# The second payload copy of a scatter moved from GpSimd, in halves, to ScalarE, in one instruction

## The chip, the cores and the metric

The kernel runs on one core of a Trainium2 chip. Its engines work side by side, each with its own queue of instructions: TensorE (matmul, PE in the profile), VectorE (DVE), ScalarE (ACT), GpSimd (POOL) and SyncE (SP), which issues most DMAs. The metric is the device time of one execution in microseconds.

## The reference

A macaron layer: a mixture-of-experts feed-forward block, tiled attention, and the same feed-forward block again, on 16 x 512 tokens of 128 numbers.

```python
x = L0_attn_batch                                   # (16, 512, 128)
x = x + 0.5 * _L0_ffn_ref(_layernorm(x), ...)
x = x + _L0_attn_ref(_layernorm(x), ...)
x = x + 0.5 * _L0_ffn_ref(_layernorm(x), ...)

# in _L0_ffn_ref, for the tokens x_aD and 8 experts, of which each token has 2:
scores_aE = x_aD @ router_DE
topv_aK, topi_aK = jax.lax.top_k(scores_aE, TOP_K)
gates_Ea = jax.nn.sigmoid(masked_aE).T              # zero for experts not chosen
routed_in_EaD = x_aD[None, :, :] * gates_Ea[:, :, None]
h_EaF = silu(routed_in @ w_in_eDF) * (routed_in @ w_swiglu_eDF)
out_aD = silu(x @ w_in_sh.T) * (x @ w_sw_sh.T) @ w_out_sh.T + sum_e(h_EaF @ w_out_eFD)
```

## The kernel before

The kernel has five stages, each a block of its own, and a stage begins when all engines have ended the one before:

1. Normalise and route (lines 316 to 703). 16 blocks (NB) of 512 tokens (BT = 4 tiles of 128). For each block the tokens are normalised, the router's scores are made, the two best experts are found, each token's row in the list of each of its experts is worked out, and the tokens are scattered to the list `pairs` in memory, once for either expert. Meanwhile the shared feed-forward part is computed.
2. Experts (L798, `experts(0)`): 71 loads of 256 rows from `pairs`, the expert's matmuls, results scattered back.
3. Attention, with the routing of the second feed-forward block.
4. Experts again (`experts(1)`), and the sum.

What the change touches is in the first stage. `PAY` is the payload: a ring of RB = 4 blocks, and for each block two copies (c = 0 and 1) of 4 rows of 128 numbers with a destination and a gate behind them. VectorE's `norm(b)` (L513) writes the first copy with four instructions of L520, and raises `normed`. For b >= 4 it first waits (L517) until all 8 scatters of block b - 4 have landed, since it writes over their payload. VectorE then finds the experts (`dve_top`, `dve_pick`), writes destination and gate to both copies (`gate`, L524, raising `gated`) and the row numbers `POS` (`dve_place`, L239, raising `placed`). `low` (L536) and `weights_low` (L589) are subtractions with both inputs in SBUF that stand in the same queue.

GpSimd's `second(b, h)` (L399) copies the 128 numbers of two tiles from the first payload to the second, L403, a half block each time, and raises `pay1`. `scatter(b, h)` (L405) issues the 4 indirect DMAs of the same half (2 tiles x 2 experts, L412), 8 for a block, 128 in all. The order is written out by hand in lines 416 to 428: second(0, 0); then for each block second(b, 1), scatter(b, 0), second(b + 1, 0), scatter(b, 1). So a copy stands ahead of every four scatters. The stage's last step on GpSimd is the wait until all scatters have landed.

ScalarE's order is a loop over i from -2 to 15 (L472): `high(i + 1)` (L456), in some rounds `deviation` (a square root, with a table load before and after, L444 and L445), `silu(i, 0)`, `gate(i + 1)` (L460), `copy(i + 2)` (L451, which takes the transposed block out of PSUM), in the first round `deviation(1)`, then `silu(i, 1)`. `deviation(1)` gives what `norm(1)` to `norm(3)` need. `silu` is L465, and waits for the shared part's matmuls (L643 to L645). `copy(b)` waits for TensorE's `turn(b)`, which itself waits for `normed`.

Of the kernel before, what the change touches and what calls it, by code (L numbers as in the profile page):

```python
# [10 lines left out]
ACT = mybir.ActivationFunctionType  # L11
# [4 lines left out]
BT = 4  # L16
# [23 lines left out]
def macaron(nc, batch, wq, bq, wk, bk, wv, bv, wo, bo, router, w_in_sh, w_out_sh, w_sw_sh,  # L40
            w_in_e, w_sw_e, w_out_e, out):
    B, S, D = batch.shape
    E, _, F = w_in_e.shape
    N = B * S
    T = N // P
    NB = T // BT
# [17 lines left out]
    RB = 4  # L64
# [13 lines left out]
    with ExitStack() as ctx:  # L78
        def sb(name, shape, dt=F32, mem=ctx):
            return mem.enter_context(nc.sbuf_tensor(name, shape, dt))  # L80
# [235 lines left out]
        with ExitStack() as mem, nc.Block() as block:  # L316
            PAY = sb("PAY1", [P, RB, TOPK, BT, ROW], mem=mem)
# [46 lines left out]
            def _(pool):  # L364
# [31 lines left out]
                                          base=0, pattern=[[1, E], [-1, E]], channel_multiplier=0))  # L396
                st.did(pool.tensor_copy(tile_no[:, :], tile_i[:, :]))

                def second(b, h):  # L399
                    half = slice(h * BT // 2, (h + 1) * BT // 2)  # L400
                    if h == 0:
                        pool.wait_ge(k["normed"], b + 1)
                    pool.tensor_copy(PAY[:, b % RB, 1, half, 0:D], PAY[:, b % RB, 0, half, 0:D]).then_inc(k["pay1"], 1)  # L403

                def scatter(b, h):  # L405
                    if h == 0:
                        pool.wait_ge(k["gated"], b + 1)
                        pool.wait_ge(k["placed"], b + 1)
                    pool.wait_ge(k["pay1"], 2 * b + h + 1)
                    for j in range(h * BT // 2, (h + 1) * BT // 2):  # L410
                        for c in range(TOPK):
                            pool.indirect_dma_start(  # L412
                                pairs, bass.IndirectOffsetOnAxis(ap=POS[:, b % RB, j, c:c + 1], axis=0),
                                PAY[:, b % RB, c, j, :], None).then_inc(scattered1[b % RB], 16)

                second(0, 0)
                for b in range(NB):
                    second(b, 1)
                    scatter(b, 0)
                    if b + 1 < NB:  # L420
                        second(b + 1, 0)
                    scatter(b, 1)
                    if b == 1:
                        pool.wait_ge(k["pads_written"], 16)
                        st.did(pool.iota(ints[:, :], pattern=[[P, 2 * E]], base=PADS, channel_multiplier=1))
                        st.settle()
                        pool.tensor_copy(pad_rows[:, :, D:D + 1].bitcast(I32), ints[:, :].unsqueeze(2))\
                            .then_inc(k["consts"], 1)
# [4 lines left out]
            def _(act):  # L433
# [13 lines left out]
                def copy(b):  # L447
                    act.wait_ge(k["xt_turned"], b + 1)
                    if b >= RB:
                        act.wait_ge(k["xt_split"], b - RB + 1)  # L450
                    act.activation(XT1[:, b % RB, :], bank[0][:, :], ACT.Copy).then_inc(k["xt_copied"], 1)  # L451

                def high(b):
                    if b >= RB:
                        act.wait_ge(k["up1"], b - RB + 1)
                    act.activation(XTH[:, b % RB, :], bank[0][:, :], ACT.Copy).then_inc(k["xt_high"], 1)  # L456
# [15 lines left out]
                for i in range(-2, NB):  # L472
# [7 lines left out]
                        gate(i + 1)  # L480
                    if 0 <= i + 2 < NB:
                        copy(i + 2)
                    if i == -2:
                        deviation(1)
                    if 0 <= i < NB:
# [500 lines left out]
        with ExitStack() as mem, nc.Block() as block:  # L986
            PAY = sb("PAY2", [P, AB, TOPK, BT, ROW], mem=mem)
# [547 lines left out]
```

## Time and profile before

| | |
|---|---|
| median of 3 runs | 972.58 us (965.75 to 974.33) |
| the profiled execution | 966.89 us, span 965.1 us |
| TensorE busy | 831.0 us (86%) |
| VectorE busy | 645.5 us (67%) |
| ScalarE busy | 571.7 us (59%) |
| GpSimd busy | 648.7 us (67%) |
| mean granted TensorE clock | 0.935 of full speed |

The shares are means over stages with different limits. The first stage lasts to about 204 us; what limits it is read from its own rows. The busy time of GpSimd counts the making of a scatter's descriptors, not the landing of its data.

### The profile page before, as it was taken

Reading aid. Unit: us, or ns where it says so; the run is one execution under the profiler, and the core shown is the slowest. Engines: PE = TensorE matmul, PEld = TensorE weight load, DVE = VectorE, ACT = ScalarE, POOL = GpSimd, SP = SyncE. Lnnn points to the kernel's source line nnn. Section 1 sums busy time; section 2 is a strip of 40 time slices with the busy share of each in tenths; the row PEclk is TensorE's granted clock in tenths of the full one; section 3 lists DMA queues with packets and bytes.
Section 4 is the critical chain, followed back from the end, with each engine's and each line's share of the span. In section 5 each row is a group of like instructions: output and inputs, shape, how many; then the busy total and the mean of one; then the engine's idle time right before and its main releaser. Section 6 shows DMA issues by size and latency. Waiting matters only on the chain. (4 is left out here: it accounts for less than half of the span.)

```text
span 965.1 us, 19487 instructions
## 1 busy us (share of the span) xinstructions
PE 831.0 (86%) x5857; PEld 728.5 (75%) x5857; DVE 645.5 (67%) x2022; ACT 571.7 (59%) x1662; POOL 648.7 (67%) x701
## 2 busy tenths in 40 slices
PE   4787877539999999279999999996499999998997
PEld 3676766439999999236777767775399999997776
DVE  6786756426666666157899999885466666664775
ACT  3324232027777777189988889872177777774332
POOL 4878887817777777470688877677457777776431
PEclk9997887859999999789999999997799999999999
DMA  9611111323333333250112211111423333332863
GB/s 241 192 50 49 45 48 48 94 59 95 103 108 103 109 103 98 71 168 8 51 57 80 81 34 40 40 42 40 110 74 106 105 100 106 104 103 74 237 171 101
DMA packets 112920, 88.01 MB, mean 91 GB/s; under 512 B 13426, under 2 KB 102132, under 8 KB 112820
## 3 DMA queue, kind: packets, MB, share of 16 engines
q1 hardware_dynamic: 94816, 51.08, 20.6%
q0 software_dynamic: 17280, 35.69, 11.0%
q8 instruction: 51, 0.84, 0.4%
q14 instruction: 49, 0.40, 0.1%
q10 hardware_dynamic: 724, 0.01, 0.0%
HBM read 43.68 MB, written 43.04 MB: 90 GB/s over the span
## 5 line engine op out<-in xcount | busy, mean ns | idle before, releaser
L876 POOL DMA_INDIRECT results<-YO,XS x284 | 277.2, 976 | 120.6 <-issue 85.1
L855 DVE TENSOR_TENSOR HT<-bank,SG 128x512 f32<-128x512 f32 x142 | 98.2, 692 | 127.2 <-PE bank L950 127.0
L948 PE MATMUL bank<-XSH,WX 128*128 128x256 f32 x568 | 174.1, 306 | 0.3 <-DVE WX L864 0.3
L1056 POOL DMA_INDIRECT pairs<-PAY,POS x128 | 134.3, 1050 | 59.0 <-issue 28.8
L949 PE MATMUL bank<-XSL,WX 128*128 128x256 f32 x568 | 162.2, 286 | 0.0
L950 PE MATMUL bank<-XSH,WX 128*128 128x256 f32 x568 | 162.0, 285 | 0.0
L412 POOL DMA_INDIRECT pairs<-PAY,POS x128 | 131.5, 1028 | 44.7 <-issue 31.9
L966 PE MATMUL bank<-WOE,HT 128*128 x1136 | 150.3, 275 | 0.1
L966 PEld LDWEIGHTS bank<-WOE,HT 128*128 128x128 f32 x1136 | 138.1, 192 | 0.7 <-issue 0.7
L904 ACT ACTIVATE XG<-XS 128x128 f32<-128x128 f32 x284 | 111.2, 393 | 43.4 <-DMA XS<-pairs 43.0
L923 ACT ACTIVATE SG<-bank 128x512 f32<-128x512 f32 x142 | 84.9, 598 | 47.1 <-PE bank L950 46.7
L948 PEld LDWEIGHTS bank<-XSH,WX 128*128 128x128 f32 x568 | 110.2, 194 | 1.1 <-issue 1.1
L949 PEld LDWEIGHTS bank<-XSL,WX 128*128 128x128 f32 x568 | 110.7, 195 | 0.0
L950 PEld LDWEIGHTS bank<-XSH,WX 128*128 128x128 f32 x568 | 110.2, 194 | 0.0
L864 DVE CAST WX<-WE 128x1024 fp32r x142 | 99.1, 698 | 0.0
L1279 ACT ACTIVATE PR<-bank,NM 128x128 f32<-128x128 f32 x256 | 90.6, 380 | 1.0 <-DVE NM L1099 1.0
L465 ACT ACTIVATE SSG<-bank 128x512 f32<-128x512 f32 x32 | 19.1, 595 | 109.0 <-PE bank L645 109.0
L861 DVE TENSOR_TENSOR XSL<-bank,XSH 128x256 fp32r<-128x256 f32 x142 | 59.0, 415 | 33.3 <-ACT XSH L909 33.1
L956 PE MATMUL bank<-ident,XG 128*128 128x128 f32 x284 | 55.9, 280 | 29.4 <-ACT XG L904 29.4
L915 ACT ACTIVATE YO<-bank 128x256 f32<-128x256 f32 x142 | 54.6, 385 | 34.2 <-PE bank L966 33.8
L1427 PEld LDWEIGHTS bank<-V,PT 128*128 128x128 f32 x512 | 63.2, 195 | 6.7 <-issue 6.7
L1403 PE MATMUL bank<-KT,QT 128*128 128x512 f32 x128 | 65.7, 596 | 2.4 <-ACT PR L1279 2.1
(197 smaller groups left out, 1747.4 us busy)
## 6 DMA issues: line engine op xcount, KB each, us to landing
XS<-pairs SPq DMA_DIRECT2D x142, 130.0 KB
Y<-results SPq DMA_DIRECT2D x32, 256.0 KB, 3.2
YF<-results SPq DMA_DIRECT2D x32, 256.0 KB, 3.7
results<-YO,XS POOLq DMA_INDIRECT x284
pairs<-PAY,POS POOLq DMA_INDIRECT x256, 2.3
out<-X SPq DMA_DIRECT2D x16, 256.0 KB, 2.6
pairs<-pad_rows SPq DMA_DIRECT2D x16, 130.0 KB, 3.9
pairs<-pad_rows SPq DMA_DIRECT2D x1, 1040.0 KB, 14.3
```

Of the source, the lines that this page charges most:

```text
L412: pool.indirect_dma_start(pairs, bass.IndirectOffsetOnAxis(ap=POS[:, b % RB, j, c:c + 1], axis=0), PAY[:, b % RB, c, j, :], None).then_inc ...
L855: dve.tensor_tensor(HT[:, i % 2, :], bank[4 + i % 2][:, :], SG[:, i % 2, :], ALU.mult)\
L864: dve.tensor_copy(WX[:, i % 2, :, :].rearrange("p h f -> p (h f)"), WE[:, ds(e * 4 * F, 4 * F)]).then_inc(k["e_weights"], 1)
L876: pool.indirect_dma_start(results, bass.IndirectOffsetOnAxis(ap=XS[:, u, j, AT_DEST:AT_DEST + 1].bitcast(U32), axis=0), YO[:, u, j, :], No ...
L904: act.activation(XG[:, i % 2, j, :], XS[:, slot(i), j, 0:D], ACT.Copy, scale=XS[:, slot(i), j, AT_GATE:AT_GATE + 1]).then_inc(k["xs_scaled ...
L923: act.activation(SG[:, i % 2, :], bank[2 + i % 2][:, :], ACT.Silu).then_inc(k["e_silu"], 1)
L948: pe.matmul(ps, WX[:, i % 2, 1, w], hi, start=True, stop=False)
L949: pe.matmul(ps, WX[:, i % 2, 0, w], lo, start=False, stop=False)
L950: mm = pe.matmul(ps, WX[:, i % 2, 0, w], hi, start=False, stop=True)
L966: mm = pe.matmul(chunk(bank[6 + i % 2], j), HT[:, i % 2, (2 * c + j) * P:(2 * c + j + 1) * P], WOE[:, ds(e * FC * D + c * D, D)], start=(c ...
L1056: pool.indirect_dma_start(pairs, bass.IndirectOffsetOnAxis(ap=POS[:, b % AB, j, c:c + 1], axis=0), PAY[:, b % AB, c, j, :], None).then_inc ...
L1279: ins = act.activation(PR[:, b % 2, a, g * P:(g + 1) * P], chunk(bank[4 + a % 2], g), ACT.Exp, bias=NM[:, b % 2, a, g:g + 1], accum_out=SU ...
```

## The change

`second` goes from GpSimd's program to ScalarE's. There it is one instruction for a whole block (128 x 512 numbers instead of twice 128 x 256), raises `pay1` by one for a block, and stands right behind `copy(i + 2)` in every round. GpSimd's wait for `pay1` is now one for a block, ahead of the first scatter.

```diff
-                def second(b, h):
-                    half = slice(h * BT // 2, (h + 1) * BT // 2)
-                    if h == 0:
-                        pool.wait_ge(k["normed"], b + 1)
-                    pool.tensor_copy(PAY[:, b % RB, 1, half, 0:D], PAY[:, b % RB, 0, half, 0:D]).then_inc(k["pay1"], 1)
-
                 def scatter(b, h):
                     if h == 0:
+                        pool.wait_ge(k["pay1"], b + 1)
                         pool.wait_ge(k["gated"], b + 1)
                         pool.wait_ge(k["placed"], b + 1)
-                    pool.wait_ge(k["pay1"], 2 * b + h + 1)
                     for j in range(h * BT // 2, (h + 1) * BT // 2):
...
-                second(0, 0)
                 for b in range(NB):
-                    second(b, 1)
                     scatter(b, 0)
-                    if b + 1 < NB:
-                        second(b + 1, 0)
                     scatter(b, 1)
...
+
+                def second(b):
+                    act.wait_ge(k["normed"], b + 1)
+                    act.activation(PAY[:, b % RB, 1, :, 0:D], PAY[:, b % RB, 0, :, 0:D], ACT.Copy).then_inc(k["pay1"], 1)
...
                         copy(i + 2)
+                        second(i + 2)
                     if i == -2:
                         deviation(1)
```

## Rows read from the trace of the kernel before

**Rows 1.** Groups by line of GpSimd, 19.3 to 198.7 us: busy us, mean ns | idle

```profile
L412 POOL DMA_INDIRECT pairs<-PAY,POS x128 | 131.5, 1028 | 44.7 <-issue 31.9 <-DVE POS L239 10.1 <-POOL PAY L403 2.5
L403 POOL COPY PAY<-PAY 128x256 f32<-128x256 f32 x30 | 12.8, 426 | 0.1
```

**Rows 2.** Timeline (start us, us, instruction [idle before]): first and last scatter

```profile
19.34 1.15 POOL L412 DMA_INDIRECT pairs<-PAY,POS  x1 [10.10 <-DVE POS L239]
...
197.65 0.97 POOL L412 DMA_INDIRECT pairs<-PAY,POS  x1 [0.30 <-issue]
```

**Rows 3.** Timeline of VectorE: row numbers of blocks 0, 2, 15; last norm; last addition

```profile
18.19 0.22 DVE L239 TENSOR_REDUCE POS<-PICK 128x8 uint32<-128x64 f32 x1
...
39.53 0.22 DVE L239 TENSOR_REDUCE POS<-PICK 128x8 uint32<-128x64 f32 x1
...
155.79 1.11 DVE L520 TENSOR_SCALAR PAY<-X,MV,RST 128x128 f32<-128x128 f32 x4 [5.19 <-DMA pairs<-PAY,POS]
...
169.93 0.22 DVE L239 TENSOR_REDUCE POS<-PICK 128x8 uint32<-128x64 f32 x1
...
186.80 0.69 DVE L546 SCALAR_TENSOR_TENSOR X<-bank,X 128x512 f32<-128x512 f32 x1 [2.21 <-PE bank L655]
```

**Rows 4.** Timeline of the step from the first stage to the experts

```profile
203.88 4.81 SPq L894 DMA_DIRECT2D XS<-pairs  x8
...
206.80 0.69 PE L956 MATMUL bank<-ident,XG 128*128 128x128 f32 x2 [20.04 <-ACT XG L904]
```

**Rows 5.** Waits, 0 to 200 us: us in total, times, longest

```profile
ACT SSG L465 <- PE bank L645: 109.0, 28, 9.0
...
DVE PAY L520 <- DMA pairs<-PAY,POS: 16.7, 5, 5.2
```

**Rows 6.** Timeline of GpSimd: block 11's last scatter; first of both last halves

```profile
153.47 0.96 POOL L412 DMA_INDIRECT pairs<-PAY,POS  x1 [0.30 <-issue]
...
188.74 0.98 POOL L412 DMA_INDIRECT pairs<-PAY,POS  x1 [0.17 <-issue]
...
193.84 0.97 POOL L412 DMA_INDIRECT pairs<-PAY,POS  x1 [0.30 <-issue]
```

**Rows 7.** Timeline of GpSimd: a copy between scatters; block 2's first scatter

```profile
28.74 0.96 POOL L412 DMA_INDIRECT pairs<-PAY,POS  x1 [0.30 <-issue]
29.70 0.40 POOL L403 COPY PAY<-PAY 128x256 f32<-128x256 f32 x1
30.27 1.11 POOL L412 DMA_INDIRECT pairs<-PAY,POS  x1 [0.17 <-issue]
...
42.00 0.99 POOL L412 DMA_INDIRECT pairs<-PAY,POS  x1 [0.22 <-issue]
```

**Rows 8.** Timeline of ScalarE: shortest gap ahead of a silu; the SBUF copy

```profile
39.38 0.60 ACT L465 ACTIVATE SSG<-bank 128x512 f32<-128x512 f32 x1 [1.08 <-PE bank L645]
...
89.65 3.61 ACT L489 ACTIVATE WE<-stage 128x4096 fp32r<-128x4096 f32 x1
```

**Rows 9.** Timeline of ScalarE, 8 to 13 us: the first round

```profile
10.32 1.28 ACT L444 ACT_TABLE_LOAD   x1
12.00 0.30 ACT L444 ACTIVATE SD<-MV,eps_c 128x12 f32<-128x12 f32 x1 [0.40 <-DVE MV L504]
```

**Rows 10.** Timeline of GpSimd and VectorE: scatters that meet VectorE's subtractions

```profile
106.59 1.19 DVE L589 TENSOR_TENSOR WE<-stage,WE 128x1024 fp32r<-128x1024 f32 x1
107.06 1.56 POOL L412 DMA_INDIRECT pairs<-PAY,POS  x1 [0.30 <-issue]
...
149.08 0.68 DVE L536 TENSOR_TENSOR XTL<-XTR,XTH 128x512 fp32r<-128x512 f32 x1
149.18 1.44 POOL L412 DMA_INDIRECT pairs<-PAY,POS  x1 [0.17 <-POOL PAY L403]
```

**Rows 11.** Windows: length, busy us PE, PEld, DVE, ACT, POOL; clock; DMA

```profile
100.00:198.70 98.70, 65.46 (x387) 56.10 (x386) 55.04 (x241) 20.79 (x41) 79.80 (x86) 0.82 0.21 59
...
209.00:520.00 311.00, 285.35 (x2124) 252.27 (x2125) 203.41 (x546) 233.45 (x717) 205.79 (x208) 0.95 0.30 87
```

## Prediction

> **What bounds the kernel now.** I read the page first: no engine is full over the whole span (TensorE 86%, GpSimd 67%), and its chain of work that ended last covers only the end of the kernel, so it can't say what sets the end of the first stage. That has to be read from the stage itself. The groups by line of GpSimd between 19.3 and 198.7 us [rows 1] are the main view: 128 scatters of 1.03 us make 131.5 us, 30 payload copies 12.8 us, and of the idle time 10.1 us lies ahead of the first scatter. The rest, 44.7 - 10.1 = 34.6 us, is only the step from one instruction to the next. With 0.4 us of two small instructions (L425, L427) this is 131.5 + 12.8 + 34.6 + 0.4 = 179.3 us, exactly what lies between the start of the first scatter at 19.34 and the end of the last at 197.65 + 0.97 = 198.62 [rows 2]. GpSimd never waits for data in between: it is the bound of this stage. VectorE is through with its last piece of the stage at 186.80 + 0.69 = 187.5 us [rows 3], 11.1 us before GpSimd. The next stage begins when the scatters have landed: the first load of expert rows is issued at 203.88, and TensorE works on its rows at 206.80 [rows 4]. So what GpSimd's queue loses in this stage, everything behind it should gain, until another engine is late.
>
> How far the others are behind it is seen from two more views. In the waits of the stage [rows 5] VectorE waits 16.7 us in 5 pieces for scatters to free a payload buffer (the wait in norm, L517): the producers are held back by GpSimd, not the other way round. And the row numbers of the last block are ready at 169.93 + 0.22 = 170.2 us [rows 3], while its first scatter starts at 188.74 [rows 6]: a cushion of 18.6 us.
>
> **The change, part by part.** *Removed from GpSimd: 30 copies that stand between scatters* (two more ran at 8.5 us, under the 10.1 us wait, and cost nothing). Between two plain scatters there are 0.30 us [rows 7]; where a copy stands between, the copy begins at once, takes 0.41 us (0.40 to 0.67, 12.8 us in all), and the next scatter follows 0.16 to 0.17 us later [rows 7]. The saving is so 12.8 + 30 x 0.17 - 30 x 0.30 = 12.8 + 5.1 - 9.0 = 8.9 us. The 0.30 us come back in full because that is the step that every scatter behind a scatter shows.
>
> *Removed and added waits on GpSimd.* Ahead of the first scatter of a block there were three waits (gated, placed, pay1), and there are three after; the one ahead of the second half goes. They can no longer run under a copy. The nearest row is the last block: the scatter at 193.84 has one satisfied wait and no copy ahead of it and still starts 0.30 us after the end of the one before [rows 6]. I take zero. The upper bound is the whole step after a copy once more, 0.17 us x 15 blocks = 2.6 us of loss; a gain is excluded, since the step of 0.30 us is there without any wait.
>
> *Added to ScalarE: 16 copies of 128x512 from SBUF to SBUF.* The trace has no such one; the nearest are 128x4096 in 3.61 us, SBUF to SBUF, and 128x512 from PSUM in 0.60 us [rows 8]. By columns alone the first gives 3.61 / 8 = 0.45 us; the second says 0.60, and has the same shape. I take 0.60, with 0.45 as the lower end and as much above, 0.75, as the upper. That is 16 x 0.60 = 9.6 us of ScalarE work, all of it in ScalarE's idle time: the new copy stands between copy(i+2) and silu(i, 1), and ScalarE waits 109.0 us for TensorE ahead of the 32 silus (28 waits) [rows 5]. The shortest idle time between a copy of the transposed block and the next silu is 1.08 us, just before 39.38 us [rows 8], so even 0.75 fits. If that cover were gone, it would cost 0.60 us a block in the producers, and they have the cushion of 18.6 us. The wait for normed in front of it is always satisfied, since the copy of the transposed block before it in the queue needed the same data: nothing is queued behind a new stall. And GpSimd's wait for pay1 never ends last: copy(b) precedes the scores from which the row numbers of b are made.
>
> *One place where the cover is short.* In the first round the new copy stands before deviation(1). ScalarE's table load starts at 10.32, right behind copy(0), ends at 11.60, and 0.40 us of slack are left before the square root [rows 9]. 0.60 - 0.40 = 0.2 us late (0.05 to 0.35), and norm(1), the ranks of block 0 and the first scatter with it: the stage starts 0.2 us late.
>
> *What shifts: the scatters against VectorE's instructions.* An undisturbed scatter takes 0.967 us, so of the 131.5 us 131.5 - 128 x 0.967 = 7.7 us are stretching. The trace shows when that happens: at 149.18 a scatter takes 1.44 us under the subtraction L536 (149.08 to 149.76), at 107.06 one takes 1.56 us under L589 (106.59 to 107.78) [rows 10]. In both, and in the other 13 that exceed 1.15 us, a VectorE instruction with two inputs in SBUF is running 0.12 us after the start of the scatter, and the scatter ends 0.85 us after the end of that instruction (149.76 + 0.86 = 150.62; 107.78 + 0.84 = 108.62). Where none is running at that moment, nothing is added. So it depends on the phase. I stepped the queue along with this rule: scatter starts 0.30 us after the last end, port needed 0.12 us after the start, VectorE's instructions where the trace has them, norm(b) not before 1.34 us after the last scatter of block b-4 (155.79 behind 153.47 + 0.96 = 154.43 for the last block [rows 3, 6]). With the copies this gives 7.9 us of stretching (7.7 seen) and an end at 197.8 (198.6 seen). Without them it gives 4.7 us and an end near 186.5. The reason is mainly that in the last blocks, where norm waits for GpSimd, L536 fell on the start of a scatter behind a copy each time (137.98, 149.18, 160.38 us, 0.47 us each), and without the copies falls between two starts. 7.9 - 4.7 = 3.2 us; I take 2.5 of it, since the small stretches are not in the stepping, with 0 and 4 as ends.
>
> On this the Trainium skill says something else. "SBUF — State Buffer", section "Who interferes with whom", has tensor_tensor contending with GpSimd's reads only, and infers that it doesn't stall descriptor generation, which needs the write interface. The rows disagree: the two scatters above are long under exactly such instructions. By the page the stretching would not follow VectorE's phase, and the sum would lack the 2.5 us.
>
> *The sum.* 8.9 + 2.5 - 0.2 = 11.2 us less in this stage. The producers allow it: with GpSimd 11 us shorter their 16.7 us of waiting shrink but don't vanish, and VectorE's end at 187.5 moves forward with the norms that waited. The profiled execution took 966.9 us (span 965.1), the median of the runs is 972.6; I take the saving off the median, since the stages behind are moved, not changed: 972.6 - 11.2 = 961.4 us, 1.15% less. Against the profiled execution it would be 955.7.
>
> **The rivals.**
>
> *A: only the copies are won.* The phase of scatters and VectorE falls as badly as before, or the stretching has another cause: the saving is 8.9 - 0.2 = 8.7 us, the time 963.9, and that is 0.9%, within 1%. For it: the stepping is fragile, and a shift of 0.1 us moves a hit. Against it: it reproduces the old stretching to 0.2 us. (The rule of "SBUF — State Buffer" of the Trainium skill, above, would give this case too; the rows so far speak against it.)
>
> *B: GpSimd becomes starved or its waits show.* The row numbers of block 2 are ready at 39.53 + 0.22 = 39.75, and the first scatter of the stage started 0.93 us after its row numbers (18.41 to 19.34) [rows 2, 3]: block 2 can start at 40.7. Without four copies before it GpSimd, which started block 2 at 42.00 [rows 7], is free at 42.00 - 4 x 0.28 = 40.9 (0.41 + 0.17 - 0.30 = 0.28 for each copy). It is the one tight place, with 0.2 us to spare; if the producers are later there by 1 us, or the three waits cost their 2.6 us, 3.6 us are lost: 11.2 - 3.6 = 7.6, time 965.0.
>
> *C: the change doesn't do what it says*, since the end of the stage is set by something else just behind GpSimd: VectorE's 187.5 us, should it not move. GpSimd would end at 198.6 - 11.2 = 187.4, so even then only 0.1 us is lost. Only a second, unseen delay in the 5.3 us between the last scatter and the first load could eat the gain; nothing in the trace speaks for it. Time 972.
>
> *D: slower.* TensorE's granted clock decides the long stages: in the first expert stage, 209 to 520 us, it is busy 285.4 of 311 us at a granted clock of 0.95, while it got 0.82 in the second half of the first stage, where it idles more [rows 11]. 1.2 and 2.4 GHz are the levels between which this mean lies. If the shifted start led to more time at the lower level, to be over 1% slower it would have to lose 9.7 + 11.2 = 20.9 us of 285.4, a mean of 0.95 / 1.073 = 0.885 instead of 0.95. Time then above 982. Against it: the work ahead of the stage and the idle gap before it (TensorE waits 20 us for the first rows [rows 4]) stay the same.
>
> **How the numbers follow.** Forecast 0.52, A 0.27, B 0.13, C 0.04, D 0.04. A change of less than 1% is about what a measurement of this kernel can't tell from none: the three runs shown lie 8.6 us apart, so the median itself may be off by 3 us. The forecast lies only 1.5 us beyond the bound of 9.7 us, so a quarter of its cases fall within 1%, and a quarter of A's fall beyond it: faster by over 1% 0.52 x 0.8 + 0.27 x 0.4 + 0.04 (larger effects of phase) = 0.57; slower 0.03; within 1% 0.40. For the range: A and B reach to 965, plus 3 us of the median's spread, 969; below, 8.9 + 4 = 12.9 of saving and 3 us of spread give 957, and 956 with a run like the fastest. The forecast's own range is 959 to 964.
>
> **What would show it.** In the changed profile: 128 scatters and no copy on GpSimd in the stage, all steps 0.30 us, also ahead of the first of a block (waits free); 16 new ScalarE instructions of 0.45 to 0.75 us, and the first scatter at about 19.5; scatters summing to 128 us or so instead of 131.5 (A: 131 or more); last scatter ending at 187 to 188; VectorE's wait for scatters down from 16.7 to about half, and its last addition well before 187; the first load 5.3 us after the last scatter; the stages after it as long as before. The prediction is wrong if a step ahead of a block's first scatter is far over 0.30 us, if GpSimd waits for row numbers in blocks 1 to 3, or if the stages behind 209 us change their length by more than 3 us.

## The result, and the profile after

The comparison of the changed kernel with the kernel before gives a ratio of 0.9882 (95%: 0.9847 to 0.9917), 1.18% faster. The forecast was 1.15%.

| | before | after |
|---|---|---|
| runs | 965.75, 966.15, 972.58, 974.33 | 952.04, 953.09, 953.88, 956.15 |
| median | 969.37 us | 953.49 us |
| profiled execution | 966.89 us | 952.04 us |
| busy PE / DVE / ACT / POOL | 831.0 / 645.5 / 571.7 / 648.7 us | 822.7 / 643.3 / 581.4 / 627.7 us |

As an absolute time the median of the four runs, 953.5 us, is below the range's low end of 956. The ratio of the two listed medians is 0.9836, outside the compared ratio's own interval; I can't account for that from the runs shown. The compared ratio is used here: 0.9882 x 972.6 = 961.1 us beside the forecast 961.4. The profiled pair lies 14.8 us apart, 1.5%. A later comparison, on chip 2, gave 0.9928, below.

GpSimd in the first stage, groups by line, 19 to 190 us (busy us, mean ns | idle), kernel after, beside [rows 1]:

```profile
L406 POOL DMA_INDIRECT pairs<-PAY,POS x128 | 126.8, 991 | 52.1 <-issue 35.9 <-DVE POS L239 15.6 <-ACT PAY L445 0.3
L417 POOL COPY pad_rows<-ints 128x16 int32<-128x16 int32 x1 | 0.2, 212 | 0.1
```

The payload copies are gone and the scatters' sum shrank from 131.5 to 126.8 us. Of the 15.6 us put down to row numbers, 13.1 lie ahead of the first scatter; the other eight are single steps of 0.30 us, as the next timeline shows. ScalarE, groups by line, 5 to 190 us:

```profile
L459 ACT ACTIVATE SSG<-bank 128x512 f32<-128x512 f32 x32 | 19.1, 596 | 95.3 <-PE bank L640 95.3
L445 ACT ACTIVATE PAY<-PAY 128x512 f32<-128x512 f32 x16 | 10.0, 628 | 0.0
```

The copy takes 0.63 us. ScalarE's wait ahead of the silus fell from 109.0 to 95.3 us [rows 5], and it is still far from full.

Timeline of the kernel after (start us, us, instruction [idle before]): the first rounds of ScalarE, the first scatter, the step around the two small instructions of L415 and L417, the largest stretched scatter, VectorE's last addition, the last scatter, and the first load of the experts.

```profile
10.16 0.62 ACT L445 ACTIVATE PAY<-PAY 128x512 f32<-128x512 f32 x1
10.81 1.28 ACT L434 ACT_TABLE_LOAD   x1
12.10 0.30 ACT L434 ACTIVATE SD<-MV,eps_c 128x12 f32<-128x12 f32 x1
...
19.47 1.15 POOL L406 DMA_INDIRECT pairs<-PAY,POS  x1 [13.12 <-DVE POS L239]
...
39.93 0.21 POOL L417 COPY pad_rows<-ints 128x16 int32<-128x16 int32 x1
40.68 0.99 POOL L406 DMA_INDIRECT pairs<-PAY,POS  x1 [0.54 <-issue]
...
112.84 0.97 POOL L406 DMA_INDIRECT pairs<-PAY,POS  x1 [0.30 <-DVE POS L239]
114.11 1.56 POOL L406 DMA_INDIRECT pairs<-PAY,POS  x1 [0.30 <-issue]
...
177.29 0.69 DVE L541 SCALAR_TENSOR_TENSOR X<-bank,X 128x512 f32<-128x512 f32 x1 [2.21 <-PE bank L650]
...
184.74 0.97 POOL L406 DMA_INDIRECT pairs<-PAY,POS  x1 [0.30 <-issue]
...
190.94 4.81 SPq L889 DMA_DIRECT2D XS<-pairs  x8
```

The square root starts 0.1 us later than in [rows 9], the first scatter 0.13 us later than in [rows 2]. Of the 127 steps between scatters one is 0.54 us, behind the two small instructions; the other 126 are 0.30 or 0.31. After the first scatter GpSimd never starves. The last scatter ends at 185.71 instead of 198.62, the first load goes 5.23 us later (5.26 before), and VectorE's last addition has moved forward as well, from 187.49 to 177.98. Waits of the kernel after, 0 to 190 us:

```profile
ACT SSG L459 <- PE bank L640: 95.3, 28, 8.7
...
DVE PAY L515 <- DMA pairs<-PAY,POS: 5.9, 2, 4.0
```

VectorE's 16.7 us in 5 waits for scatters [rows 5] are down to 5.9 in 2, a third where half was expected.

From first load to first load, and on to the end, the stages of the profiled executions last: first expert stage 199.1 us before and 197.8 after, attention 291.5 and 291.7, second expert stage 270.6 and 269.8. So 12.9 of the 14.8 us come from the first stage.

### The profile page after: what moved, and what is told of

Same layout as the page of the kernel before. It is cut to its first block and busy times, and to the rows that moved or that the text cites. A ratio compares the mean times of both kernels' runs of the same rounds, so it can differ in the third digit from the quotient of the medians.

```text
span 950.3 us, 19471 instructions
## 1 busy us (share of the span) xinstructions
PE 822.7 (87%) x5857; PEld 721.5 (76%) x5857; DVE 643.3 (68%) x2022; ACT 581.4 (61%) x1678; POOL 627.7 (66%) x669
## 3 DMA queue, kind: packets, MB, share of 16 engines
q0 software_dynamic: 17280, 35.69, 11.2%
## 5 line engine op out<-in xcount | busy, mean ns | idle before, releaser
L1051 POOL DMA_INDIRECT pairs<-PAY,POS x128 | 134.5, 1051 | 58.9 <-issue 28.7
L406 POOL DMA_INDIRECT pairs<-PAY,POS x128 | 126.8, 991 | 52.1 <-issue 35.9
L459 ACT ACTIVATE SSG<-bank 128x512 f32<-128x512 f32 x32 | 19.1, 596 | 95.3 <-PE bank L640 95.3
```

Source lines behind the costliest of these rows:

```text
L406: pool.indirect_dma_start(pairs, bass.IndirectOffsetOnAxis(ap=POS[:, b % RB, j, c:c + 1], axis=0), PAY[:, b % RB, c, j, :], None).then_inc ...
L1051: pool.indirect_dma_start(pairs, bass.IndirectOffsetOnAxis(ap=POS[:, b % AB, j, c:c + 1], axis=0), PAY[:, b % AB, c, j, :], None).then_inc ...
```

## The experiments

Four questions were open. Is the gain of the first stage the same each time? Does it come through the copies and the stretching as said? Is the stretching really caused by VectorE's instructions with two inputs in SBUF? And why did the ratio vary? The kernels ran on four chips: `after_again` and its three companions on chip 11, `low_psum`, the two `pool_` kernels and `tail_sbuf` on chip 10, the other two tails on chip 12, and the last two on chip 2. All comparisons of this section are with the kernel before on the same chip. Times of single instructions are from one profiled execution each.

### The changed kernel and three variants on chip 11

`after_again` is the changed kernel, unaltered. `act_double` makes ScalarE's copy twice, once into a spare tile:

```diff
+ act.wait_ge(act_s, b + 1)
+ act.activation(EXTRA[:, :, :], PAY[:, b % RB, 0, :, 0:D], ACT.Copy).then_inc(act_s, 1)
  act.activation(PAY[:, b % RB, 1, :, 0:D], PAY[:, b % RB, 0, :, 0:D], ACT.Copy)
```

`half_moved` is the kernel before with only a block's first half on ScalarE; the copy of the second half stays on GpSimd, in its old place:

```diff
-                second(0, 0)
                 for b in range(NB):
                     second(b, 1)
                     scatter(b, 0)
-                    if b + 1 < NB:
-                        second(b + 1, 0)
                     scatter(b, 1)
...
+ # ScalarE, behind copy(b)
+ act.activation(PAY[:, b % RB, 1, 0:BT // 2, 0:D], PAY[:, b % RB, 0, 0:BT // 2, 0:D], ACT.Copy)
```

`vector_copy` is the changed kernel with the copy on VectorE instead:

```diff
- # second(i + 2) on ScalarE
  dve.wait_ge(k["gate_raw"], b + 1)
+ dve.tensor_copy(PAY[:, b % RB, 1, :, 0:D], PAY[:, b % RB, 0, :, 0:D])
```

> The changed kernel, unaltered, as the yardstick of this chip. My theory (GpSimd's queue bounds the first stage; 8.9 us come from the copies, the rest from scatters that no longer meet VectorE's two-input subtractions) expects the last scatter to end at 185.7 us within 0.5, scatters summing to 127 us, and a ratio to the kernel before of 0.983 to 0.990. The rival that part of the gain (1.9 us of the 14.8 by the two profiles) lies behind the first stage and is real expects the first expert stage again 1.3 us shorter than before; I expect that to be scatter of single executions.

> The changed kernel with ScalarE's copy done twice in every block (the first one into a spare tile), so 16 more instructions of 0.62 us, 9.9 us of ScalarE work. My theory, that the copy lies wholly in ScalarE's idle time but for the first round, expects 0.6 us more (the first scatter at 20.1 instead of 19.47), all other stages the same: ratio to the kernel before higher than that of the unaltered changed kernel by 0.0006. The rival that ScalarE's copy is on the path of the stage expects 5 to 10 us more, and that the change as made lost as much.

> One half of the change alone: ScalarE copies the first half of each block (128x256), GpSimd keeps the copy of the second half, 15 of 128x256 between scatters, at the head of each block. By the queue theory without phase: half of the 8.9 us, last scatter at 198.6 - 4.4 = 194.2. Stepping the queue past VectorE's instructions as in the prediction gives 5.0 us of stretched scatters instead of 7.9 and an end at 191 to 192. The rival that the gain is one of a removed dependency (GpSimd waiting for its own write) and not of queue time would give the same saving for any number of copies above zero removed, so near none here.

> The copy moved to VectorE instead of ScalarE: one instruction of 128x512 ahead of destination and gate, about 0.41 us as VectorE's other SBUF copies of this size. The queue theory expects GpSimd's queue the same as in the changed kernel within 1.5 us, since VectorE has a cushion: last scatter at 186 to 187. Its instructions delay the row numbers by 0.41 us a block, of which only block 0 (first scatter at 19.9 without ScalarE's delay, so 19.8) and block 2 count: 0.5 to 1.5 us later. The rival that a VectorE copy from SBUF to SBUF locks GpSimd out for its whole length, wherever in a scatter it falls, expects 16 x 0.41 = 6.6 us more stretching.

Measured (us; on this chip the kernel before took 1066.9 in the median, against 965 to 966 on chips 2, 10 and 12). The ratio of `after_again` leaves out its longest run, 1088.95, which is also the profiled one; the other three have a median of 1074.6.

| | median | ratio (95%) | first scatter | scatters in sum | last scatter ends | first load |
|---|---|---|---|---|---|---|
| after_again | 1079.2 | 1.0104 (1.0028 to 1.0181) | 19.59 | 125.2 | 231.9 | 240.2 |
| act_double | 1081.0 | 1.0148 (1.0087 to 1.0210) | 20.05 | 127.3 | 227.9 | 236.2 |
| half_moved | 1075.7 | 1.0104 (1.0040 to 1.0167) | 19.21 | 127.3 | 218.0 | 233.6 |
| vector_copy | 1076.1 | 1.0098 (1.0063 to 1.0133) | 19.25 | 126.5 | 235.0 | 242.3 |

None of them gains here, and the three ends that were expected for the last scatter (185.7, 191 to 194, 186 to 187) were missed by more than 23 us. Timeline of `after_again`, GpSimd, 60 to 75 us:

```profile
63.44 0.96 POOL L406 DMA_INDIRECT pairs<-PAY,POS  x1 [0.30 <-issue]
72.70 0.96 POOL L406 DMA_INDIRECT pairs<-PAY,POS  x1 [8.30 <-DVE POS L239]
```

Waits of the same, 60 to 230 us:

```profile
ACT SSG L459 <- remote: 87.6, 10, 17.3
DVE SC L209 <- remote: 59.5, 6, 14.6
POOL pairs L406 <- DVE POS L239: 44.8, 8, 8.5
```

and the end of its first stage:

```profile
230.97 0.97 POOL L406 DMA_INDIRECT pairs<-PAY,POS  x1 [0.31 <-issue]
...
238.45 0.69 DVE L541 SCALAR_TENSOR_TENSOR X<-bank,X 128x512 f32<-128x512 f32 x1 [2.21 <-PE bank L650]
240.15 4.81 SPq L889 DMA_DIRECT2D XS<-pairs  x8
```

The scatters are as short as anywhere, but GpSimd waits for row numbers (8.3 us here; the longest steps in the other three traces are 7.7 to 8.9 us), and the first load goes 1.0 us after VectorE's last addition, 8.2 us after the last scatter. In all four the step from last scatter to first load is over 7 us, 15.6 us in `half_moved`. GpSimd alone isn't the bound of these four kernels on this chip; that it wasn't of the kernel before either is likely, but no trace shows it. The first two wait rows show where the producers stand: a silu and the copy of the router's scores wait up to 17.3 and 14.6 us for TensorE's results, where the profile finds no instruction of the core that ended just then ("remote"). At 56.25 us the last matmul ahead of a silu is recorded as over, and the silu starts at 64.06. All four traces from this chip have such waits, 82 to 94 us ahead of the silus, and none of the others has one. What holds TensorE's results back isn't in the rows. From 60 to 100 us TensorE got a granted clock of 0.67 and did 117 matmul records of work, against 0.83 and 189 in the same stretch of the kernel after on its own chip. What makes this chip slow in the first and the expert stages (the first expert stage took 237.5 us, attention 294.0) isn't settled, and since no trace of the kernel before is there from it, nor are the 1.0 to 1.5% by which all four are longer. What follows from the variants is little: the doubled copy delays the first scatter by 0.46 us and changes the total within the overlap of the intervals (1.0148 against 1.0104), and the copy on VectorE costs no more there than on ScalarE (1.0098). As tests of the split into terms the four are inconclusive, since the term they should vary wasn't on the path.

### Where the copies stand on GpSimd: pool_head and pool_late

Both are the kernel before with one copy of 128x512 for a block on GpSimd instead of two of 128x256, either ahead of a block's first scatter or between its sixth and seventh:

```diff
+ second(0)                          # both
  for b in range(NB):
-     second(b, 1)
-     scatter(b, 0)                  # 4 indirect DMAs
-     second(b + 1, 0)
-     scatter(b, 1)
+     scatter(b, 0, 4)               # pool_head: tiles 0 to 3
+     second(b + 1)
...
+     scatter(b, 0, 3)               # pool_late: tiles 0 to 2
+     second(b + 1)
+     scatter(b, 3, 4)
```

> The kernel before with one copy of the whole block (128x512) on GpSimd, ahead of the block's 8 scatters. The length of such a copy on GpSimd isn't in the trace; twice 0.41 less some fixed part, 0.62 to 0.82 us. Work on GpSimd is the same as in the next run, only its place differs. Stepping the queue gives 5 to 7.6 us of stretched scatters (L536 falls on the start of a scatter in the blocks where norm waits for GpSimd) and an end at 196.5 to 197. The rival without phase expects exactly the end of the next run.

> As the run before it, but the whole-block copy stands between the 6th and 7th scatter of the block before. Stepping the queue gives 4.5 to 5 us of stretched scatters and an end at 193.4 (copy of 0.62 us) to 195.8 (0.75): 1 to 3 us less than with the copy at the head. The rival without phase expects the same sum of scatters in both.

Measured: `pool_head` 970.1 us, ratio 1.0043 (1.0003 to 1.0084), last scatter's end at 202.6; `pool_late` 966.8, ratio 1.0004 (0.9958 to 1.0050), last scatter's end at 192.6. Groups by line of GpSimd in the first stage, `pool_head`:

```profile
L410 POOL DMA_INDIRECT pairs<-PAY,POS x128 | 125.9, 984 | 57.8 <-issue 36.2 <-POOL PAY L401 11.3 <-DVE POS L239 10.2
L401 POOL COPY PAY<-PAY 128x512 f32<-128x512 f32 x15 | 9.6, 642 | 0.0
```

and `pool_late`:

```profile
L410 POOL DMA_INDIRECT pairs<-PAY,POS x128 | 126.2, 986 | 47.1 <-issue 34.5 <-DVE POS L239 10.2 <-POOL PAY L401 2.3
L401 POOL COPY PAY<-PAY 128x512 f32<-128x512 f32 x15 | 9.8, 650 | 0.0
```

I had expected the two to differ by 1 to 3 us and in stretching, by the phase in which the scatters behind a copy meet VectorE. They don't differ in stretching (125.9 and 126.2 us), and both ends lie outside what was expected: 196.5 to 197 for `pool_head`, 193.4 to 195.8 for `pool_late`. They differ in the step behind the copy. Timeline, `pool_head`:

```profile
144.77 0.62 POOL L401 COPY PAY<-PAY 128x512 f32<-128x512 f32 x1
146.20 0.98 POOL L410 DMA_INDIRECT pairs<-PAY,POS  x1 [0.81 <-POOL PAY L401]
```

and `pool_late`:

```profile
146.91 0.62 POOL L401 COPY PAY<-PAY 128x512 f32<-128x512 f32 x1
147.69 0.98 POOL L410 DMA_INDIRECT pairs<-PAY,POS  x1 [0.16 <-POOL PAY L401]
```

In `pool_head` the three waits of a new block (gated, placed, pay1) stand directly between copy and scatter, and the step is 0.81 us; in `pool_late` none stands there, and it is 0.16. That happens 14 times: 14 x 0.65 = 9.1 us of the 10.0 between the two ends. It isn't the number of waits. In the kernel before the same three waits stand between a copy and a block's first scatter too, and the step is 0.17 us ([rows 7], the copy at 29.70), as it is in `half_moved` (0.16). The difference is what pay1 waits for. In the kernel before a block's first scatter needs only the block's first half, whose copy was over four scatters earlier, so the wait is satisfied; in `pool_head` it needs the copy that GpSimd has made just before, and the profile names that copy as what ended the 0.81 us. So a satisfied wait costs nothing behind a scatter or behind a copy; a wait for the instruction directly ahead of it cost 0.65 us. This is read from three kernels beside each other; no run changed this wait alone.

Both ends also follow GpSimd's sums. Against the kernel before `pool_late` has 5.3 us less of scatters, 3.0 less of copies and 2.3 more of steps, and ends 6.0 earlier; `pool_head` has 5.6 and 3.2 less and 13.0 more, and ends 4.0 later (202.6 against 198.6).

`pool_late` shows a second thing: its first stage ended 6.0 us earlier than before (first load at 197.86 instead of 203.88), and yet the whole took as long. That is followed up below.

### What stretches a scatter: low_psum and three tails

`low_psum` is the kernel before with the first input of `low` read from PSUM (and TensorE's next transposes waiting until it has been read):

```diff
- dve.tensor_tensor(XTL[:, b % RB, :], XT1[:, b % RB, :], XTH...
+ dve.tensor_tensor(XTL[:, b % RB, :], bank[0][:, :], XTH...
+ pe.wait_ge(k["xt_split"], b)       # ahead of turn(b)
```

> The kernel before, copies on GpSimd as they were; only VectorE's subtraction L536 takes its first input from the bank in PSUM that holds the same numbers, instead of from SBUF, and the next transpose waits for it. If scatters are stretched because a VectorE instruction with two SBUF inputs is running 0.12 us after their start, the 3.95 us of stretching under this line go: last scatter at 193.4 to 195 instead of 198.6, scatters summing to 127 to 129 us. If the stretching has another cause (or, as the Trainium skill, SBUF - State Buffer, section Who interferes with whom, infers, if such an instruction does not hold up the making of descriptors), the sum stays at 131 to 132 us and the end at 198.6.

Measured: 978.2 us, ratio 1.0119 (1.0035 to 1.0203); scatters 125.4 us in sum, last end at 211.2. Groups by line of GpSimd, 19 to 215 us, `low_psum`:

```profile
L412 POOL DMA_INDIRECT pairs<-PAY,POS x128 | 125.4, 980 | 63.4 <-issue 48.8 <-DVE POS L239 11.8 <-POOL PAY L403 2.5
```

With 128 x 0.967 = 123.8 us for undisturbed scatters, the stretching is down from 7.7 to 1.6 us, although GpSimd still has all its 30 copies. The expectation of the end, 193.4 to 195, failed, for a reason of the edit's own: the added wait makes TensorE wait more than 20 us for `low`, row numbers come late, and GpSimd gets steps of up to 4.8 us. Since the starved queue also shifts the phase, this alone doesn't show the cause. The tails do it without touching the queue: the changed kernel with a run of otherwise useless 128x512 instructions of VectorE at the end of its stage, under the last scatters.

```diff
+ for n in range(9):    # tail_sbuf
+     dve.tensor_tensor(o, stage[:, 0:512], stage[:, 512:1024], ALU.subtract)
+ for n in range(9):    # tail_psum
+     dve.tensor_tensor(o, bank[0][:, :], stage[:, 512:1024], ALU.subtract)
+ for n in range(15):   # tail_copy
+     dve.tensor_copy(o, stage[:, 0:512])
```

> The changed kernel with 9 extra subtractions of 128x512 on VectorE after its last work of the first stage (178 us), both inputs in SBUF, into unused parts of a tile: about 6.2 us of 0.69 each while GpSimd makes its last six scatters and nothing else runs on VectorE. If such an instruction holds the port that a scatter needs 0.12 us after its start, nearly each of these scatters is stretched, by 0.3 us on average if VectorE lets go between instructions, so the last scatter ends 1.5 us later, or by several us if it doesn't. If it doesn't hold that port, all stay at 0.97 us.

> As the run with 9 extra subtractions at the end of VectorE's first stage, but with the first input in PSUM. All theories on two SBUF inputs expect no stretching: the last six scatters at 0.97 us, end of the last at 185.7. If any busy VectorE stretches scatters, they are stretched here too.

> As the run with extra subtractions, but with 15 copies of 128x512 from SBUF to SBUF, 0.41 us each, 6.2 us in all. The trace of before showed scatters under norm (L520, one SBUF input, 0.34 us each) longer by 0.07 to 0.14 us at most. My theory expects small stretches, 0 to 0.3 us each, end of the last scatter at 185.7 to 187. The Trainium skill (SBUF - State Buffer, section Who interferes with whom) has such a copy lock GpSimd out of the shared ports, so it would expect the scatters to wait for at least the running copy, 0.2 us each on average or more.

Timeline of GpSimd and VectorE, `tail_sbuf` (x9 groups the nine subtractions):

```profile
178.18 5.63 DVE L626 TENSOR_TENSOR stage<-stage 128x512 f32<-128x512 f32 x9
178.69 1.01 POOL L406 DMA_INDIRECT pairs<-PAY,POS  x1 [0.31 <-issue]
180.00 1.51 POOL L406 DMA_INDIRECT pairs<-PAY,POS  x1 [0.30 <-issue]
181.81 0.97 POOL L406 DMA_INDIRECT pairs<-PAY,POS  x1 [0.30 <-issue]
183.09 0.96 POOL L406 DMA_INDIRECT pairs<-PAY,POS  x1 [0.30 <-issue]
```

`tail_psum`:

```profile
177.55 3.79 DVE L626 TENSOR_TENSOR stage<-bank,stage 128x512 f32<-128x512 f32 x6
177.55 0.96 POOL L406 DMA_INDIRECT pairs<-PAY,POS  x1 [0.30 <-issue]
178.82 0.97 POOL L406 DMA_INDIRECT pairs<-PAY,POS  x1 [0.30 <-DMA pairs<-PAY,POS]
180.09 0.97 POOL L406 DMA_INDIRECT pairs<-PAY,POS  x1 [0.30 <-issue]
```

`tail_copy`, GpSimd alone:

```profile
178.59 1.09 POOL L406 DMA_INDIRECT pairs<-PAY,POS  x1 [0.30 <-issue]
179.98 1.16 POOL L406 DMA_INDIRECT pairs<-PAY,POS  x1 [0.30 <-issue]
```

With one input in PSUM nothing is stretched, although three of the scatters (178.82, 180.09 and the next, 181.36) start 0.07 to 0.15 us behind the start of a subtraction. With both in SBUF one of the four shown is by 0.54 us and one by 0.04, and how much follows from who comes first: a subtraction starts at 179.98, the scatter at 180.00, and it takes 1.51 us. The one at 178.69 meets the first subtraction 0.17 us before its end (178.18 + 0.68 = 178.86) and ends 0.84 us after it, at 179.70, as the stepping has it. The scatters at 181.81 and 183.09 start 0.09 and 0.03 us ahead of a subtraction (181.91, 183.12) and take 0.97 and 0.96. So only one was stretched by much, where the expectation had nearly each by 0.3 us, and the last ended at 186.6.

Plain copies SBUF to SBUF add 0.12 to 0.20 us to each of the four scatters that they meet, within the 0 to 0.3 expected. Three of these scatters end 0.84 us after the end of the copy that ran 0.12 us after their start, the fourth 0.91 us after it. So copies follow the same rule as the subtractions; they add less since they are shorter, and the rule isn't one of two inputs alone. The lock that the expectation names as the other reading would look the same here: each scatter is held until the running copy ends.

This is the rule that the stepping used, with one edge more exact: it isn't enough that such an instruction runs 0.12 us after the scatter's start, it must have begun before it. In the first stages of all fourteen traces a subtraction with both inputs in SBUF begins up to 0.15 us behind a scatter's start 19 times, and none of these scatters takes over 1.01 us. Where it begins 0.03 us or less ahead, both happen: 0.97 us in `after_third` (0.03 ahead), 1.51 here (0.02).

The tails' totals were 962.3 us (`tail_sbuf`; before on its chip 965.9), 958.6 (`tail_psum`; 965.3) and 962.8 (`tail_copy`; 965.3), one run each. The last scatters ended at 186.6, 187.4 and 186.6, so in the first stage they keep 11.2 to 12.0 us of the gain (`tail_psum` has two more scatters of 1.44 and 1.47 us in the middle of the stage). What differs more is the next stage.

### Where a gain of the first stage is lost again

The windows of the first expert stage, from first load to first load (length, busy us PE, PEld, DVE, ACT, POOL; clock; DMA). Kernel before:

```profile
203.88:402.98 199.10, 184.81 (x1562) 183.66 (x1562) 115.64 (x213) 138.13 (x355) 137.82 (x142) 0.95 0.34 96
```

After:

```profile
190.94:388.76 197.82, 183.50 (x1562) 182.35 (x1562) 115.67 (x213) 138.21 (x355) 137.84 (x142) 0.97 0.35 97
```

`pool_late`, and then `tail_copy`:

```profile
197.86:404.72 206.86, 186.62 (x1562) 183.44 (x1562) 120.15 (x213) 131.87 (x355) 146.03 (x142) 0.95 0.33 92
```

```profile
191.79:398.36 206.57, 186.76 (x1562) 183.85 (x1562) 121.20 (x213) 132.15 (x355) 145.26 (x142) 0.95 0.33 92
```

The code of this stage is the same in all four. Yet it takes 198 to 199 us in two and 207 us in the others, at a granted clock of 0.95 like the kernel before. GpSimd's busy time rises most, from 138 us to 146 for the same 142 scatters of results (VectorE's by 4.5 to 5.5 us). And GpSimd's queue fills this stage as it fills the first. In the kernel after (whole line of the stage):

```profile
L871 POOL DMA_INDIRECT results<-YO,XS x142 | 137.8, 971 | 59.9 <-issue 42.4 <-ACT YO L910 16.9 <-DMA results<-YO,XS 0.6
```

137.8 + 59.9 = 197.7 of the 197.8 us, and of the idle time 16.9 us is one wait, for the first results; the rest is steps of 0.30. The same line and the waits for rows in `pool_late`:

```profile
L873 POOL DMA_INDIRECT results<-YO,XS x142 | 146.0, 1028 | 60.7 <-issue 37.5 <-ACT YO L912 22.6 <-DMA results<-YO,XS 0.6
```

```profile
ACT XG L901 <- DMA XS<-pairs: 52.8, 34, 22.3
```

and one place of its timeline:

```profile
321.31 0.69 DVE L861 CAST WX<-WE 128x1024 fp32r x1
321.36 1.47 POOL L873 DMA_INDIRECT results<-YO,XS  x1 [0.31 <-issue]
```

It is the same mechanism in another place: the cast of the next expert's weights begins 0.05 us before a scatter, which then takes 1.47 us. Of the 20 scatters over 1.15 us in this stage 12 have such a cast running 0.12 us after their start; for the other 8 the rule of the tails doesn't serve (7 have an instruction with an input in PSUM there, L852 or L858, and one has none). A load of rows may only start when the results of its slot have landed, so the loads come late: ScalarE waits 34 times for rows, in the kernels before and after 2 times (23.8 and 20.4 us, nearly all of it for the first).

It isn't a choice between two lengths. The other traces lie between:

| | expert stage | scatters of results | of these over 1.15 us |
|---|---|---|---|
| before, after, before_again, after_third, pool_head, low_psum (first) | 197.8 to 199.1 us | 137.8 to 137.9 us | 1 |
| tail_psum (first) | 200.1 | 140.2 | 4 |
| tail_sbuf (first) | 202.8 | 141.5 | 8 |
| tail_copy (first) | 206.6 | 145.3 | 18 |
| pool_late (first) | 206.9 | 146.0 | 20 |
| before (second) | 270.6 | 139.4 | 4 |
| before_again (second) | 275.4 | 145.1 | 19 |

The stage is longer by about what its scatters are stretched. The last two lines are the unaltered kernel before: it too lost 5 us in one of its two traces, so this isn't a cost of the change, but a spread that a gain of one stage can be lost in or enlarged by. What decides how the two queues meet isn't shown. It isn't the stage's start alone: in `after_third` it begins at 191.75 us and takes 198.4, in `tail_copy` at 191.79 and takes 206.6. That the casts cause the whole 8 us is argued from these rows; no run changed the cast alone. On chip 11 the first expert stage has 37 to 44 such scatters (152 to 154 us in sum), which is 14 to 16 of the 38 to 40 us by which it is longer there.

### How steady the gain is: both kernels again

> The kernel before, unaltered, so that there is a trace of it from the same chip and session as the next run. Two cases. Where the whole kernel takes about 966 us, as in the first measurement, I expect the last scatter of the first stage at 198.6 within 1 us and GpSimd never waiting for row numbers. Where it takes about 1067 us, as on the chip on which the changed kernel came out 1% longer, the theory that there the producers (TensorE and what follows it) bound the stage, so that GpSimd's saved time is only idle time, expects GpSimd to wait for row numbers here too, by about 60 - 13 = 45 us over the stage. The rival that the change itself slows the producers there expects few such waits and a stage shorter by 8 us or more than that of the changed kernel.

> The changed kernel beside the run before. Where the whole takes about 966 us: last scatter at 185.7 within 1 us, the first load of the experts 12.9 us earlier than in the run before, ratio 0.984 to 0.992, with the rest decided by whether scatters and VectorE's casts meet in the expert stages (198 us for the first one where they don't, up to 207 where they do). Where it takes about 1067: ratio 1.00 to 1.01, GpSimd waiting for row numbers for 50 us or more, and the first stage's end within 8 us of the other kernel's.

Both ran on chip 2. `before_again` 965.4 us, ratio to the kernel before 0.9987 (0.9960 to 1.0013), as it must be. `after_third` 958.0 us, ratio 0.9928 (0.9901 to 0.9954). Groups by line of GpSimd in the first stage, first `before_again`, then `after_third`:

```profile
L412 POOL DMA_INDIRECT pairs<-PAY,POS x128 | 131.3, 1026 | 44.7 <-issue 31.9 <-DVE POS L239 10.1 <-POOL PAY L403 2.5
L403 POOL COPY PAY<-PAY 128x256 f32<-128x256 f32 x30 | 12.8, 426 | 0.1
```

```profile
L406 POOL DMA_INDIRECT pairs<-PAY,POS x128 | 127.8, 998 | 51.9 <-issue 36.5 <-DVE POS L239 15.1 <-DMA pairs<-PAY,POS 0.3
```

The first is [rows 1] again to 0.2 us, with long scatters in the same places (138.05, 149.26, 160.49): the stretching isn't noise, it is fixed by the order of the queues. The last scatter ends at 198.17 and 186.51, the first loads go at 203.40 and 191.75: 11.65 us, where 12.9 were expected. The difference is in the stretching: here it fell by 3.5 us, not by 4.7, since in `after_third` a scatter at 159.03 still meets a subtraction (1.47 us). Of the 11.65 us only 7.5 are left in the medians, and the ratio is just outside the expected 0.984 to 0.992. The six runs of `after_third` lie in two groups, 952.9, 953.4 and 956.4, and 959.6, 960.1 and 960.3; the profiled one is of the first (first expert stage 198.4 us). The spread has the size of what the expert stages showed above (the profiled `before_again`, 969.8 us, has its 275.4 us in the second one), but the upper group has no trace, so this is likely and not shown.

## Why the prediction was right, point by point

**What bounds the stage: right.** GpSimd's queue set the end of the first stage, and 12.9 us out of it moved everything behind by 12.9 us (last scatter 198.62 to 185.71, first load 203.88 to 190.94). The limit of this reading is shown by chip 11, where the row numbers come late and the same change wins nothing.

**The copies, 8.9 us: right.** Steps came back at 0.30 us in 126 of 127 places. The exception is behind L417, where the new step is 0.54 instead of 0.22: 0.3 us that the sum didn't have.

**The moved waits cost nothing: right.** The first scatter of every block but block 2 starts 0.30 us after the one before, also with three waits ahead of it, as the row of the last half said. A nearer row was there: in [rows 7] the same three waits stand behind a copy, at a step of 0.17 us. The 0.65 us of `pool_head` is another case, a wait for the copy just made. The change can't meet it, since the copy is no longer in GpSimd's queue.

**The copy on ScalarE, 0.60 us each and hidden: right.** 0.63 us, 10.0 us in sum; the waits ahead of the silus fell by 13.7 us. The head start lost was 0.13 us, where 0.2 had been taken.

**The stretching, 2.5 us: the mechanism right, the size too small.** The scatters' sum fell by 4.7 us (131.5 to 126.8), with an excess over 128 x 0.967 of 3.0 us instead of 7.7. That is over the upper end of 4, and the sum is below the 128 that was named as the sign. The stepping had said 3.2 and named the three regular hits (137.98, 149.18, 160.38), which are gone. I discounted it to 2.5 for small stretches, and that was no reason: scatters of up to 1.15 us make 0.9 us of the excess before and 0.7 after, and the 15 longer ones fell from 6.9 to 2.4 us (7 are left). The second pair of traces gives 3.5 us, within the ends, so about 1 us of it differs from one pair of executions to the other. The stage's sum is then 8.9 + 4.7 - 0.1 - 0.3 = 13.2 us beside the 12.9 measured at the last scatter's end, which so came at 185.7 and not at 187 to 188. Rival A, with its 131 us or more of scatters, is out, and so is the rule of "SBUF — State Buffer" in the Trainium skill, section "Who interferes with whom" (inferred there), by which the stretching wouldn't follow such instructions: 1.51 us against 0.97 with only the place of one input changed, at like phases.

**Starvation at block 2 (rival B): didn't happen.** The prediction had the block's rows ready for a scatter at 40.7 and GpSimd free at 40.9; its first scatter starts at 40.68, with the 0.54 us step in front of it, which the profile puts down to no wait. The margin was as thin as reckoned.

**TensorE's clock (rival D): didn't happen.** The stretch of 209 to 520 us that the prediction calls the first expert stage [rows 11] reaches 117 us into attention; the stage itself ends at 402.98. In the kernel after the stage had a granted clock of 0.97 instead of 0.95, and it explains none of the loss where one is seen: `pool_late` had 0.95, as before.

**The stages behind are as long as before: right in the pair of profiles, not in general.** 197.8 against 199.1, 291.7 against 291.5, 269.8 against 270.6. The prediction had named over 3 us as what would prove it wrong, and in `pool_late` and `tail_copy` the first expert stage is 7.5 to 7.8 us longer, in the kernel before itself the second one 4.8 us longer from one trace to the other. This is the rival I lacked: not a wait or a clock, but the same meeting of scatters and VectorE one stage on. By the rows above it likely decides whether the 11.7 to 12.9 us of the first stage arrive whole, and it is a likely reason that one comparison gave 0.9882 and another 0.9928.

**The total: right within its range, the close agreement luck.** The compared ratio meets the forecast within 0.03%, but its own interval reaches from 0.83 to 1.53% faster, the two listed medians give 1.64%, the profiled pair 1.5% and chip 2 0.72%. The sum of 11.2 us was for the first stage, which gained 12.9 in one pair and 11.65 in the other.

## What to carry to other kernels

When a queue of indirect DMAs sets the end of a stage, take everything else out of it, and sum what stands between two DMAs from the timeline: the instruction and its steps, not the instruction alone. Then look at which of the DMAs are long, and at what VectorE had begun just before each: a regular hit is a term of the sum with its own sign, and moving one input to PSUM or shifting the phase removes it (in `low_psum` the wait that this needed cost more than it gave). A gain in one stage arrives whole only if the stages behind keep their length; compare that length in several executions and variants before counting the gain.

## What the runs showed of the hardware that was not expected

- On GpSimd satisfied waits cost nothing: three of them stand behind a copy at a step of 0.17 us, and behind an indirect DMA at 0.30, as without any. A wait for the copy directly ahead makes the step 0.81 us.
- An indirect scatter of 128 rows takes 0.97 us, and up to 1.66 us in the kernel before (2.00 in `vector_copy`) if VectorE has begun a subtraction with both inputs in SBUF before it. It then ends about 0.84 us after that instruction. Copies and casts from SBUF to SBUF did the same (1.09 to 1.16 us in `tail_copy`, 1.47 in `pool_late`). If the scatter begins first, even by 0.03 us, nothing is added by a subtraction.
- One stage with the same instructions took 198 to 207 us, and at the same granted clock of 0.95 both 199 and 207. Its scatters over 1.15 us went from 1 to 20 with it.
- One of four chips ran the kernel in 1067 us instead of 966. In the four traces from it GpSimd stands idle for up to 8.9 us at a time in the first stage, mostly for row numbers, behind results of TensorE that come late for a reason that no row shows, and a saving on GpSimd won nothing.
